# Two-layer conditional MLP on one core: the opening is reordered (one chunk of x ahead of layer 0's weights, first tile by feature chunks)

## The reference, cut to what matters

```python
def reference(x, itok_B_0_63, itok_B_0_2, W, b, wi, wo, swi, swo, g1, g2):
    # x (2, 1024, 256); W (64, 256, 256); wi (5, 256, 1024), wo (5, 1024, 256); swi, swo (2, ...)
    x = x + einsum('bsd,bdh->bsh', x, W[cat]) + b[cat][:, None, :]          # layer 0
    s0, s1 = relu(x @ swi[0]) @ swo[0], relu(x @ swi[1]) @ swo[1]           # layer 1, two shared
    eo = relu(x @ wi[type]) @ wo[type]                                      # and one selected MLP
    w = softmax(relu(concat([eo[:, 0], s0[:, 0], s1[:, 0]]) @ g1) @ g2)
    return x + eo * w[:, 0] + s0 * w[:, 1] + s1 * w[:, 2]
```

## Time and profile before

| | before |
|---|---|
| median of 3 runs | 271.71 us (271.42 to 271.82) |
| profiled execution | 271.66 us |
| its span | 269.8 us |
| PE busy | 265.1 us (98% of the span) |
| DVE, ACT, POOL busy | 160.9, 148.2, 160.8 us |

### The profile page before, as it was taken

How to read it: one execution, slowest core, us unless ns; L and a number is a source line. 1 busy time by engine, 2 the same in 40 slices (tenths; PEclk the granted TensorE clock), 3 DMA queues, 4 the chain that set the end, 5 groups by cost and what they waited for, 6 DMA issues and landing times.

```text
span 269.8 us, 3491 instructions
## 1 busy us (share of the span) xinstructions
PE 265.1 (98%) x1182; PEld 220.3 (82%) x1182; DVE 160.9 (60%) x241; ACT 148.2 (55%) x257; POOL 160.8 (60%) x170
## 2 busy tenths in 40 slices
PE   8999999999999999999999999999999999999994
PEld 8788887888888888888888888888888888888884
DVE  3879958635644444654445565345566477685684
ACT  2597357665565655665655653745644555645320
POOL 0179989999948949938944724724725528524000
PEclk9999999999999999999999999999999999999999
DMA  6735322022012022102022112112012022000008
GB/s 193 247 106 155 117 78 79 7 75 79 6 74 78 6 73 78 58 24 78 2 78 78 34 46 78 33 46 79 19 61 78 2 78 75 2 0 2 0 12 299
DMA packets 7328, 18.30 MB, mean 68 GB/s; under 512 B 1168, under 2 KB 1936, under 8 KB 7312
## 3 DMA queue, kind: packets, MB, share of 16 engines
q1 hardware_dynamic: 6592, 16.92, 18.4%
q10 hardware_dynamic: 720, 1.18, 1.4%
HBM read 16.00 MB, written 2.10 MB: 67 GB/s over the span
## 4 chain that ended last, share of the span: by engine, by line
PE 96%; DMA 2%; SPq 1%; DVE 0%; issue 0%; ACT 0%; DVEq 0%
PE acc L657 48%; PE chain L657 24%; PE right L657 12%; PE left L657 7%; PE acc L674 4%; DMA w_raw<-cat_w 2%; PE corner L657 1%; SPq L222 1%; PE left L813 0%; DVE x L648 0%; ACT w_hi L352 0%; PE left L819 0%; SPq L224 0%; DVEq L647 0%
## 5 line engine op out<-in xcount | busy, mean ns | idle before, releaser
L264 POOL TENSOR_TENSOR m_lo<-staged,m_hi 128x512 fp32r<-128x512 f32 (+1 forms) x48 | 81.5, 1706 | 80.5 <-ACT m_hi L340 65.7
L657 PE MATMUL acc<-h_hi,m_hi 128*128 128x512 f32 x190 | 73.9, 389 | 0.0
L657 PE MATMUL acc<-h_hi,m_lo 128*128 128x512 f32 x190 | 73.9, 389 | 0.0
L657 PE MATMUL acc<-h_lo,m_hi 128*128 128x512 f32 x190 | 73.9, 389 | 0.0
L364 ACT COPY kept<-chain 128x512 f32<-128x512 f32 x66 | 38.8, 588 | 57.8 <-PE chain L657 57.8
L657 PEld LDWEIGHTS acc<-h_hi,m_lo 128*128 128x128 f32 x190 | 35.7, 188 | 7.4
L657 PEld LDWEIGHTS acc<-h_hi,m_hi 128*128 128x128 f32 x190 | 35.7, 188 | 7.4
L657 PEld LDWEIGHTS acc<-h_lo,m_hi 128*128 128x128 f32 x190 | 35.7, 188 | 7.4
L471 DVE SCALAR_TENSOR_TENSOR h_lo<-left,h_hi 128x512 fp32r<-128x512 f32 x24 | 16.6, 692 | 29.9 <-ACT h_hi L376 29.9
L264 POOL TENSOR_TENSOR staged<-staged 128x128 f32<-128x128 f32 x66 | 30.9, 482 | 1.7
L476 DVE TENSOR_TENSOR left<-left,kept 128x512 f32<-128x512 f32 x22 | 15.3, 698 | 26.7 <-PE left L657 26.7
(11 more groups left out here) (107 smaller groups left out, 442.7 us busy)
## 6 DMA issues: line engine op xcount, KB each, us to landing
staged<-mlp_w SPq DMA_DIRECT2D x22, 512.0 KB, 3.3
x<-x_t ACTq DMA_DIRECT2D x4, 256.0 KB, 3.9
staged<-mlp_w SPq DMA_DIRECT2D x4, 256.0 KB, 3.3
x<-x_t SPq DMA_DIRECT2D x4, 256.0 KB, 5.4
out_t<-x SPq DMA_DIRECT2D x2, 512.0 KB, 3.3
g_sb<-g SPq DMA_DIRECT2D x1, 768.0 KB, 3.8
out_t<-x SPq DMA_DIRECT2D x3, 256.0 KB, 3.0
w_raw<-cat_w SPq DMA_DIRECT2D x4, 128.0 KB, 3.1
```

Of the source, the lines that this page charges most:

```text
L264: return nc.gpsimd.tensor_tensor(out, a, b, ALU.subtract)
L657: last = nc.tensor.matmul(out[:, columns], half[:, slot, at:at + P], moving[:, columns], start=(start and n == 0), stop=(stop and n == 2), ...
```

## The change

On SP, the second chunk of x(0,0) is requested between the two halves of w(0), and group 0's wi part is no longer requested there. ACT requests only the first chunk of x(0,0) at the start; it reads the expert number into a register of its own, waits until that chunk has landed, requests the two chunks of x(0,1), rounds the first half of w(0), requests group 0's wi part, and rounds the second half. Group 0's wi part is rounded and subtracted in two halves (`row1_hi_ready`, `row1_split`), the first before `part_hi_of(1)`. POOL takes over the subtraction for x(0,1,1). DVE handles tile (0,0) chunk by chunk, with w's subtraction in between. PE does 11 warm-up matmuls in place of 16. Tile (0,0) goes by input chunk i first and output half d second; the other tiles do the eight matmuls with x_hi first and the four with x_lo last. `direct(0, 0)` waits in three steps. The number of layer matmuls is the same.

```diff
-WARMUP = 16
+WARMUP = 11
...
+        def load_wi(eng, bank, j):
+            eng.dma_start(staged[:, j % 2, A11:RAW_S], group_weights(bank, j, slice(A11, RAW_S))).then_inc(staged_loaded[j % 2], 16)
...
-                eng.dma_start(staged[:, j % 2, A11:RAW_S], group_weights(bank, j, slice(A11, RAW_S))).then_inc(staged_loaded[j % 2], 16)
+                if j:
+                    load_wi(eng, bank, j)
...
+                    if b == d == 0:
+                        load_x(sp, 0, 0, 1)
...
-            split_first(0, False)
+            pool.wait_ge(x_hi_ready[0], 2)
+            subtract(x_part(x_lo, 0, 1, 1), x1_part(0, 1, 1), x_part(x_hi, 0, 1, 1).bitcast(F32)).then_inc(x_split[0][1][1], 1)
+
+            pool.wait_ge(row1_hi_ready, 1)
+            subtract(m_lo[:, 0, A11:A22], staged[:, 0, A11:A22], m_hi[:, 0, A11:A22].bitcast(F32)).then_inc(row1_split, 1)
+            pool.wait_ge(m_hi_ready, first_part(0))
+            subtract(m_lo[:, 0, A22:RAW_S], staged[:, 0, A22:RAW_S], m_hi[:, 0, A22:RAW_S].bitcast(F32)).then_inc(m_split, 1)
...
-            load_x(act, 0, 0)
+            load_x(act, 0, 0, 0)
 
             act.wait_ge(ones_ready, 1)
             nc.scalar.activation(table[:], ones[:, 0:1], ACT.Relu)
-            load_x(act, 0, 1)
+            mlp = act.value_load(mlp_ids[0:1, 0:1], min_val=0, max_val=EXPERTS - 1)
+
+            act.wait_ge(x_loaded[0][0][0], 16)
             for d in range(DC):
-                w_hi_of(0, d)
+                load_x(act, 0, 1, d)
+            w_hi_of(0, 0)
+            load_wi(act, bass.ds(mlp, 1), 0)
+            w_hi_of(0, 1)
             for d in range(DC):
                 x_hi_of(0, 1, d)
-            split_first_hi(0, False)
             part_hi_of(0)
+            act.wait_ge(staged_loaded[0], 16)
+            nc.scalar.copy(m_hi[:, 0, A11:A22], staged[:, 0, A11:A22]).then_inc(row1_hi_ready, 1)
             part_hi_of(1)
+            nc.scalar.copy(m_hi[:, 0, A22:RAW_S], staged[:, 0, A22:RAW_S]).then_inc(m_hi_ready, 1)
...
-            for d in range(DC):
                 w_lo_of(0, d)
-            for d in range(DC):
-                x_lo_of(0, 1, d)
+            x_lo_of(0, 1, 0)
...
+            def layer0_first():
+
+                for i in range(DC):
+                    pe.wait_ge(w_hi_ready, i + 1)
+                    pe.wait_ge(x_split[0][0][i], 1)
+                    for d in range(DC):
+                        layer0_product(0, 0, i, d, w_hi, x_hi, i == 0, False)
+                        layer0_product(0, 0, i, d, w_hi, x_lo, False, False)
+                        if d == 0:
+                            pe.wait_ge(w_split[0], i + 1)
+                        last = layer0_product(0, 0, i, d, w_lo, x_hi, False, i == DC - 1)
+                        if i == DC - 1:
+                            last.then_inc(layer0_done, 1)
+
+            def layer0(b, t):
+
+                for i in range(DC):
+                    if t == 0:
+                        pe.wait_ge(w_hi_ready, b * DC + i + 1)
+                        pe.wait_ge(w_split[b], i + 1)
+                    pe.wait_ge(x_hi_ready[b], b * t * DC + i + 1)
+                    for d in range(DC):
+                        layer0_product(b, t, i, d, w_hi, x_hi, i == 0, False)
+                        layer0_product(b, t, i, d, w_lo, x_hi, False, False)
+                for d in range(DC):
+                    for i in range(DC):
+                        if d == 0:
+                            pe.wait_ge(x_split[b][t][i], 1)
+                        last = layer0_product(b, t, i, d, w_hi, x_lo, False, i == DC - 1)
+                    last.then_inc(layer0_done, 1)
...
-                if j == i == 0:
-                    pe.wait_ge(part_split, 2)
+                if j == i == 0:
+                    pe.wait_ge(row1_split, 1)
+                    pe.wait_ge(part_split, 1)
+                elif i == 0 or j == 0 and i == 1:
+                    pe.wait_ge(m_split, first_part(j))
```

More of the change, by code:

```diff
@@ L121, in build @@
         x_first_hi = sem("x_first_hi")
-        x_split = [[sem(f"x_split{b}{t}") for t in range(HALVES)] for b in range(B)]
+        x_split = [[[sem(f"x_split{b}{t}{d}") for d in range(DC)] for t in range(HALVES)] for b in range(B)]
         w_hi_ready = sem("w_hi_ready")
@@ L135, in build @@
         m_hi_ready = sem("m_hi_ready")
+        row1_hi_ready = sem("row1_hi_ready")
+        row1_split = sem("row1_split")
         m_split = sem("m_split")
@@ L173, in part_no, with load_x @@
             return PARTS.index((*tile, d))
-        def load_x(eng, b, t):
-            for d in range(DC):
-                eng.dma_start(x1_part(b, t, d), x_t[b][:, d, t * TOK:(t + 1) * TOK]).then_inc(x_loaded[b][t][d], 16)
+        def load_x(eng, b, t, d):
+            eng.dma_start(x1_part(b, t, d), x_t[b][:, d, t * TOK:(t + 1) * TOK]).then_inc(x_loaded[b][t][d], 16)
         def group_weights(bank, j, columns):
             return mlp_w[bank, j % GROUPS:j % GROUPS + 1, :, columns].rearrange("a k p n -> p (a k n)")
+        def load_wi(eng, bank, j):
+            eng.dma_start(staged[:, j % 2, A11:RAW_S], group_weights(bank, j, slice(A11, RAW_S))).then_inc(staged_loaded[j % 2], 16)
         def load_group(eng, bank, j):
             if j < DIRECT:
-                eng.dma_start(staged[:, j % 2, A11:RAW_S], group_weights(bank, j, slice(A11, RAW_S))).then_inc(staged_loaded[j % 2], 16)
+                if j:
+                    load_wi(eng, bank, j)
                 eng.dma_start(staged[:, j % 2, WO:A11], group_weights(bank, j, slice(WO, A11))).then_inc(wo_loaded[j], 16)
@@ L241, in _ @@
                         for t in range(HALVES):
-                            load_x(sp, 1, t)
+                            for d in range(DC):
+                                load_x(sp, 1, t, d)
                         load_layer0(1)
@@ L310, in _ @@
                 pool.wait_ge(x_hi_ready[1], d + 1)
-                subtract(x_part(x_lo, 1, 0, d), x1_part(1, 0, d), x_part(x_hi, 1, 0, d).bitcast(F32)).then_inc(x_split[1][0], 1)
+                subtract(x_part(x_lo, 1, 0, d), x1_part(1, 0, d), x_part(x_hi, 1, 0, d).bitcast(F32)).then_inc(x_split[1][0][d], 1)
             split_first(0, True)
@@ L554, in x_lo_of @@
                 dve.wait_ge(x_hi_ready[b], b * t * DC + d + 1)
-                subtract(x_part(x_lo, b, t, d), x1_part(b, t, d), x_part(x_hi, b, t, d).bitcast(F32)).then_inc(x_split[b][t], 1)
+                subtract(x_part(x_lo, b, t, d), x1_part(b, t, d), x_part(x_hi, b, t, d).bitcast(F32)).then_inc(x_split[b][t][d], 1)
             nc.vector.memset(ones[:], 1.0).then_inc(ones_ready, 1)
@@ L561, in _ @@
                 dve.wait_ge(x_first_hi, d + 1)
-                subtract(x_part(x_lo, 0, 0, d), x1_part(0, 0, d), x_part(x_hi, 0, 0, d).bitcast(F32)).then_inc(x_split[0][0], 1)
-            for d in range(DC):
+                subtract(x_part(x_lo, 0, 0, d), x1_part(0, 0, d), x_part(x_hi, 0, 0, d).bitcast(F32)).then_inc(x_split[0][0][d], 1)
                 w_lo_of(0, d)
-            for d in range(DC):
-                x_lo_of(0, 1, d)
+            x_lo_of(0, 1, 0)
             dve.wait_ge(bias_loaded[0], 16)
@@ L659, in three, with layer0_product @@
                 return last
-            def layer0(b, t, d):
-                for i in range(DC):
[L663 to L676, removed]
+            def layer0_product(b, t, i, d, w, x, start, stop):
+                if b and start:
+                    pe.wait_ge(x1_ready, t * DC + d + 1)
+                at = i * D + d * P
+                return nc.tensor.matmul(acc[t][d][:], w[:, b, at:at + P], x_part(x, b, t, i), start=start, stop=stop)
@@ L686, in direct @@
                 slot = j % SLOTS
-                if i == 0:
+                if j == i == 0:
+                    pe.wait_ge(row1_split, 1)
+                    pe.wait_ge(part_split, 1)
+                elif i == 0 or j == 0 and i == 1:
                     pe.wait_ge(m_split, first_part(j))
-                if j == i == 0:
-                    pe.wait_ge(part_split, 2)
                 if j == 0 and i == 2:
@@ L702, in direct @@
                 three(hidden[i], m_hi, blocks[0], slot, *moving[0], True, False)
+                if j == i == 0:
+                    pe.wait_ge(part_split, 2)
                 three(hidden[i], m_hi, blocks[1], slot, *moving[1], False, True).then_inc(direct_done, 1)
@@ L784, in _ @@
                 nc.tensor.matmul(left[:, 0:P], ones[:], ones[:], start=True, stop=True)
[L785 to L790, removed]
+            layer0_first()
+            layer0(0, 1)
             for j in range(DIRECT):
@@ L793, in _ @@
                     direct(j, i)
-            layer0_of(1)
+            for t in range(HALVES):
+                layer0(1, t)
             for u in range(8):
```

## The result

The changed kernel takes 272.18 us (median, 271.73 to 272.74) against 271.76 for the kernel before: ratio 1.002, 95% interval 1.0012 to 1.0027. It is slower by 0.4 us: little, about the 0.2% that the prediction took for the limit, but the interval leaves out no change at all. I had forecast 270.6 in a range of 269.7 to 271.6, and faster with a chance of 0.74. The profiled execution took 272.15, span 270.0.

A forecast was written before the change was run, and what follows sets the result against it. TensorE was taken to bound the kernel, with 96% of the chain. An earlier start of 1.64 us less waits of 0.35 and 0.15 gave 1.1, taking the median from 271.71 to 270.6, range 269.7 to 271.6.

The forecast's parts named there:

- What bounds the kernel: Whole kernel: TensorE carries 96% of the chain, so products starting earlier shorten the total unless PE meets a new wait.
- Part 1: Start: the first half of layer 0's weights lands 2.2 us after its request, at 4.9, and is rounded by 5.4.
- Part 2: Start: eleven warm-ups hold PE until 5.92, clock rises at 6.26; effective start 6.09 against 7.73, a gain of 1.64 us.
- Part 3: Tile (0,0), second halves: the weights land at 6.0, or 6.9 behind a ScalarE chunk, and nothing waits.
- Part 4: Behind tile (0,0): PE waits for DVE, 0.35 us at direct(0,2) and 0.15 at output(0,1) in batch 1.
- Nothing else gives it back: Group 2, batch 1's x_lo, POOL's extra subtraction and SP's later requests: no further loss.
- (d): Start: weights do not come sooner, PE idles before its first product and the clock falls; about 274.3 us, chance 0.07.

The follow-up runs named there:

- the combined version: Changed kernel with both x(0,0) chunks requested by ScalarE at the start, group 0's wi by SP, no ScalarE register load, both later PE waits removed: 270.50 us, ratio 0.9961.
- the version with the weights first: Changed kernel with the second chunk of x(0,0) requested by SP behind both weight halves instead of between them: 273.03 us, ratio 1.0048 to the kernel before.
- the run with the second tile later: Changed kernel with the two chunks of x(0,1) requested only after the first weight half has landed: 272.82 us, ratio 1.0044 to the kernel before.

## Why the prediction was wrong, point by point

- **What bounds the kernel** held inside the span: PE carried the chain, and the ledger closes on its gaps. That the 1.9 us outside the span would stay was taken over without a reason; they became 2.2. Against the forecast of 270.5 for the profiled execution the measured 272.15 is 1.65 more: +1.7 for the hole, -0.6 for the earlier start, +0.3 for the two later waits (0.78 against 0.50) and +0.3 outside the span.
- **Part 1** held to a tenth: 2.2 us for the first half of the weights, landed at 4.9.
- **Part 2**: the start was 5.37, not 5.92, since in this execution the clock rose early and the warm-up ended at 5.14. Weight loads of the kernel after in 1.5:3.8 and 4.1:4.8:

```profile
L827 PEld LDWEIGHTS left<-ones 128*128 128x128 f32 x13 | 2.8, 328 | 0.0
...
L827 PEld LDWEIGHTS left<-ones 128*128 128x128 f32 x8 | 1.0, 192 | 0.0
```

  It was within the bounds given, and it did not matter, as the warm-up of 16 shows.
- **Part 3 is the step that failed.** "512 KB after 3.7, about 2 us at the measured rate", and then: "Nothing waits." The rate of 250 GB/s came from a stretch with four chunks queued one behind the other. The change takes that queue apart. With single requests, the rate from 2.5 to 6.5 was 142 to 212 GB/s, the weights landed at 7.97 instead of 6.0 to 6.9, and PE lost 1.7 us. The sum by rate also has no term for a request's own delay: 128 KB at 250 GB/s are 0.5 us, and the first half took 2.2. With two chunks requested at the start (the combined version) the engines were 0.90 busy in the same microsecond and the hole did not appear.
- **Part 4** had both places and both mechanisms; the first price was right and the second too small: 0.38 and 0.40 against 0.35 and 0.15. The chain through DVE has the meeting with POOL in it (1.01 for a subtraction of 0.69). The Trainium skill (SBUF — State Buffer, "Who interferes with whom") says that a VectorE instruction with two SBUF inputs contends with a GpSimd one that reads SBUF; by that rule, the trace agrees. The two experiments that take these waits out gained 0.37 and 0.59 alone, 0.72 together, with the reserve on the 0.37 made above.
- **Nothing else gives it back** held from group 2 on, and was wrong about SP: its register load stretched, and group 0's wo part was requested at 8.73, in the kernel before at 6.96. Nobody waited for it in the changed kernel.
- **Rivals.** The one on the other side, (d), had PE idle before its first product. The real one is PE idle before its seventh, which no rival had. The fear in (d), a clock that falls in the hole, came true in the version with the weights first.
- By the medians the gains do not quite add: 0.72 and 0.56 taken back singly, 1.68 together. The remaining 0.4 is not clear of the noise. By the ratios they add (0.0032 and 0.0026, 0.0059 together), and so they do in the profiles: group 2 starts 1.02 and 0.60 earlier than in the changed kernel with one set of edits, 1.64 earlier with both.

## What to carry to other kernels

When requests are reordered to bring one operand forward, price the whole train: the rate of 250 GB/s, read where four chunks were queued, did not hold for single requests, which got some 150, and the operand that comes next in the program matters as much as the first. An early first product was worth nothing here, because the second set was late; put the start back on purpose (here a longer warm-up) to see whether it carries anything. Before undoing a change, look for the waits that it left: with two of them removed and the requests packed again, the same idea gave 1.1 us. And compare the spans as well as the times: 0.3 us of this loss lay outside everything that the chain shows.

## What the runs showed of the hardware that was not expected

- The moment at which TensorE's clock rises moved between executions that begin with the same warm-up matmuls: at most 3.0 us after the first warm-up load in one (loads at 192 ns from 4.1 on, row above), 5.0 to 5.3 us after it in the kernel before, and 6.1 in the run with the second tile later, whose products were 0.40 to 0.57 apart until 7.18 and 0.23 from there. The Trainium skill (TensorE: Matmul & The Clock Gate, "What you observe") has around 4 us with 500 ns of scatter; these runs scatter more widely.
- After a gap of 2.85 us from product to product (2.45 of it idle in the profile) the clock was at its 1.2 GHz level, in the version with the weights first. After one of 2.06 us (1.67 idle), in the second profile of the changed kernel, it was not: from the second product on they came 0.23 apart. This is one execution of each.
- The time of a register load from memory varies much while transfers run: SP's pair for the expert number took 0.85 and 0.89 us before, 1.57 and 1.88 after. The transfer engines' share does not order them: it was 0.78 to 1.02 around the shorter pair, and 0.51 to 1.09 around the longer. What does is open.
